# Reordered ACT and DVE work in a self-attention loop, and a reordered first projection, in a fused fp32 Perceiver layer on one core

## The reference

```python
x = x + cross_attention(layernorm(x), ctx)      # 16 heads, 4096 context rows, int8 fake-quant
x = x + self_attention(layernorm(x))            # below
x = x + ffn(layernorm(x))                       # h = silu(gate) * up; out = h @ w_down.T
...
# self-attention: NH, NKV, D = 16, 4, 128; QPG = 4 query heads for each key head
qkv = jnp.einsum('bsh,ph->bsp', x, weight_qkv).reshape(b, s, NKV, GROUP)
scores = jnp.einsum('bsgqd,btgd->bgqst', q, k) * scale
scores = jnp.where(causal, scores, jnp.finfo(scores.dtype).min)
attn = jax.nn.softmax(scores, axis=-1)
out = jnp.einsum('bgqst,btgd->bsgqd', attn, v).reshape(b, s, NH * D)
return jnp.einsum('bse,he->bsh', out, weight_proj)
```

## Time and profile before

| what | value |
|---|---|
| median of 3 runs | 643.45 us (641.19 to 646.16) |
| the profiled execution | 641.48 us |
| its span | 639.7 us (1.78 us lie around it) |
| PE busy | 602.2 us, 94% of the span |
| DVE, ACT, POOL busy | 369.5, 299.4, 228.6 us |
| mean granted TensorE clock | 0.976 of full speed |

### The profile page before, as it was taken

One profiled execution on the slowest core, in us unless ns is written; L12 is line 12 of the kernel. 1 busy time (PEld: TensorE's weight loads), 2 busy tenths in 40 slices (PEclk: granted clock), 3 DMA queues, 4 the chain that ended last, 5 costly groups with the idle time before them and its releaser, 6 DMA issues.

```text
span 639.7 us, 12391 instructions
## 1 busy us (share of the span) xinstructions
PE 602.2 (94%) x4340; PEld 476.6 (75%) x4340; DVE 369.5 (58%) x680; ACT 299.4 (47%) x424; POOL 228.6 (36%) x120
## 2 busy tenths in 40 slices
PE   5999999999999999999999999997697999979998
PEld 3877788888887677777776777764497988769996
DVE  3796621330434778878878777766564334366652
ACT  4435232233231555555555555564247667634441
POOL 2000200000001778888788888870001544400000
PEclk9999999999999999999999999999699899979999
DMA  8664545514529655566555666600130324144510
GB/s 305 228 227 161 173 170 180 191 72 157 203 93 282 165 149 146 147 164 159 153 143 143 158 165 156 156 29 2 26 145 28 132 76 188 67 181 151 196 66 33
DMA packets 29758, 92.17 MB, mean 144 GB/s; under 512 B 5473, under 2 KB 9569, under 8 KB 23009
## 3 DMA queue, kind: packets, MB, share of 16 engines
q1 hardware_dynamic: 28480, 89.67, 45.8%
q10 hardware_dynamic: 1248, 2.10, 0.9%
HBM read 65.02 MB, written 18.35 MB: 130 GB/s over the span
## 4 chain that ended last, share of the span: by engine, by line
PE 87%; DVE 4%; ACT 3%; issue 2%; POOL 1%; DMA 1%; SPq 0%; POOLq 0%; ACTq 0%; DVEq 0%
PE ps L333 17%; PE ps L334 16%; PE ps L335 16%; PE ps L1283 11%; PE ps L1368 9%; PE ps L1380 9%; PE ps L1394 4%; POOL p_sum L574 1%; PE ps L1354 1%; PE ps L1356 1%; DMA f_ring<-stream 1%; PE ps L1549 1%; PE ps L1562 1%; ACT probs L744 1%; PE ps L1265 1%
## 5 line engine op out<-in xcount | busy, mean ns | idle before, releaser
L693 ACT ACTIVATE p_ring<-ps 128x1024 f32<-128x1024 f32 x128 | 125.7, 1022 | 103.1 <-PE ps L1368 76.2
L957 DVE TENSOR_REDUCE m_part<-ps 128x1 f32<-128x512 f32 x240 | 150.5, 684 | 30.7 <-PE ps L1283 27.9
L574 POOL TENSOR_TENSOR p_sum<-p_sum,p_ring 128x1024 f32<-128x1024 f32 x60 | 142.9, 2381 | 9.4 <-ACT p_ring L693 5.3
L1283 PE MATMUL ps<-k_stack,q_max 96*128 96x512 f32 x240 | 87.3, 424 | 1.4 <-issue 0.6
L1368 PE MATMUL ps<-q_stack,k_stack 98*128 98x256 f32 x512 | 81.5, 288 | 0.2 <-ACT p_ring L693 0.2
L1368 PEld LDWEIGHTS ps<-q_stack,k_stack 98*128 98x128 f32 x512 | 75.8, 192 | 7.8 <-ACT p_ring L693 1.2
L1380 PE MATMUL ps<-p_ring,v_head 128*32 128x256 f32 x1024 | 71.6, 383 | 0.1
L333 PE MATMUL ps<-xt_h,h_ring 128*128 128x256 f32 x208 | 60.8, 292 | 2.1 <-DVE xt_l L1071 2.1
L910 DVE SCALAR_TENSOR_TENSOR kl_buf<-ps,biases,kh_buf 128x512 fp32r<-128x512 f32 x32 | 23.9, 749 | 64.0 <-ACT kh_buf L651 63.7
L333 PE MATMUL ps<-h_ring,wkv_h 128*128 128x512 f32 x128 | 52.4, 410 | 8.2 <-DVE l_ring L870 7.2
L334 PE MATMUL ps<-xt_l,h_ring 128*128 128x256 f32 x208 | 60.1, 289 | 0.0
(11 more groups left out here) (186 smaller groups left out, 1032.4 us busy)
## 6 DMA issues: line engine op xcount, KB each, us to landing
f_ring<-stream SPq DMA_DIRECT2D x29, 1024.0 KB, 4.9
k_stack<-kh_scratch SPq DMA_DIRECT2D x60, 256.0 KB, 4.6
kh_scratch<-kh_buf SPq DMA_DIRECT2D x32, 256.0 KB, 5.5
kl_scratch<-kl_buf SPq DMA_DIRECT2D x32, 256.0 KB, 5.8
v_head<-v_all SPq DMA_DIRECT2D x16, 512.0 KB, 3.0
k_stack<-kl_scratch SPq DMA_DIRECT2D x30, 256.0 KB, 4.2
v_all<-stream SPq DMA_DIRECT2D x4, 256.0 KB, 4.6
f_ring<-stream SPq DMA_DIRECT2D x4, 256.0 KB, 5.4
```

The lines of the kernel that those rows point to most:

```text
L574: nc.gpsimd.tensor_tensor(p_sum[:, p, :], p_ring[:, 0, :] if n == 0 else p_sum[:, p, :], p_ring[:, c % 4, :], ALU.add).then_inc(sums_done, 1)
L693: nc.scalar.activation(p_ring[:, c % 4, :], ps[:, 2 * (c % 2):2 * (c % 2) + 2, :].rearrange("p b n -> p (b n)"), ACT.Exp, scale=XSCALE).th ...
L957: nc.vector.reduce_max(m_part[:, j // NT, j % NT:j % NT + 1], maximum_bank(j), AX.X).then_inc(max_read, 1)
L1283: nc.tensor.matmul(maximum_bank(j), q_max[p][0:SPLIT_ROWS, at128(j % NT)], k_stack[p][0:SPLIT_ROWS, j // NT * D:(j // NT + 1) * D], start= ...
```

## The change

There are three edits, and no arithmetic is added or removed.

1. Group 0 only: the high part of the first head's transposed probabilities is put ahead of the first half of the next queries, on ACT and on DVE.
2. Every group but the last: on ACT, `next_query(1)` moves from behind `exponential(3)` to behind `output_high(1)`, so that `normalize(3)`, `transposed_high(2)` and `output_high(1)` come first. In group 0 the second half of the rounding of slot 0 also moves behind `output_high(1)`. On DVE, `next_query(1)` moves behind `invert(3)`, `transposed_low(2)` and `output_low(1)`.
3. PE, the first 12 matmuls after the second and the third layernorm: the passes that read only `xt_h` (eight of them) come first and wait for `xth_ready`; the four that read `xt_l` come last and wait for `xtl_ready`. The sum is taken in another order.

```diff
@@ ACT, group(g)
+                transposed_high(0)
                 if first:
                     next_query(0)
-                transposed_high(0)
                 exponential(2, g)
...
                 if first:
                     half_high(0, 0)
                 exponential(3, g)
+                normalize(3, g)
+                transposed_high(2)
+                output_high(1)
+                if first:
+                    half_high(0, 1)
                 if more:
                     next_query(1)
-                normalize(3, g)
-                if first:
-                    half_high(0, 1)
-                transposed_high(2)
-                output_high(1)
-                if more:
                     half_high(1, 0)
                 else:
                     high(act, FF0, 2, uses(FF0))
@@ DVE, group(g)
+                transposed_low(0)
                 if first:
                     next_query(0)
-                transposed_low(0)
                 maximum(2, g)
...
                 output_low(0)
-                if more:
-                    next_query(1)
                 invert(3, g)
                 transposed_low(2)
                 output_low(1)
                 if more:
+                    next_query(1)
                     maximum(0, g + 1)
@@ PE, project_to_columns(w, u, to, after_norm)
                 for v in range(2):
+                    whole = to[:, v * N:(v + 1) * N]
+                    if after_norm is not None and v == 0:
+                        for kt in range(KT):
+                            if kt % 2 == 0:
+                                pe.wait_ge(xth_ready, 2 * after_norm + kt // 2 + 1)
+                            for part in (h_ring, l_ring):
+                                nc.tensor.matmul(whole, part[w][:, kt, at128(2 * u)], xt_h[:, kt, :],
+                                                 start=kt == 0 and part is h_ring, stop=False)
+                        for kt in range(KT):
+                            if kt % 2 == 0:
+                                pe.wait_ge(xtl_ready, 2 * after_norm + kt // 2 + 1)
+                            nc.tensor.matmul(whole, h_ring[w][:, kt, at128(2 * u)], xt_l[:, kt, :], start=False,
+                                             stop=kt == KT - 1)
+                        continue
                     for kt in range(KT):
-                        if after_norm is not None and v == 0 and kt % 2 == 0:
-                            pe.wait_ge(xtl_ready, 2 * after_norm + kt // 2 + 1)
-                        last = three_pass(to[:, v * N:(v + 1) * N], h_ring[w][:, kt, at128(2 * u + v)],
+                        last = three_pass(whole, h_ring[w][:, kt, at128(2 * u + v)],
```

## The result

The changed kernel ran in 631.83 us (median of 4 runs, 630.79 to 637.08), against 642.91 us for the kernel before (median of 4, 641.19 to 646.16). The ratio is 0.9866, with a 95% interval of 0.9824 to 0.9908. The intervals overlap, so a fair size for the gain is some 7 to 8.6 us, not the 11 us between the first two medians.

A forecast was written before the change was run, and what follows sets the result against it. PE, busy 94% of the span, was taken as the bound, with time won only in its idle or low-clock stretches. Terms 2.8 + 2.2 + 1.1 = 6.1 us against the 643.45 us median gave 637.5 us, range 634.5 to 642.0.

The forecast's parts named there:

- Groups 1 and 2: Fourth head of both groups: the 1.48 us gap goes and values(3) starts 1.41 us earlier, 2.8 us for two groups.
- After the two layernorms: First projections there: PE starts 0.72 us earlier, each gaining 0.36 to 0.72 us, taken as 0.54, together 1.1 us.
- both of my bounds: After both layernorms together: 0.7 us if the clock returns at the same moment, 1.4 us if its return moves along.
- Group 0: Fourth head to first projection: starts 1.63 us earlier, plus 0.56 us from faster matmuls, 2.2 us with the clock up.
- The new start: First projection in group 0: PE starts at about 496.9 us instead of 498.53, a gain of 1.63 us.
- the *new* bound: Group 0's projection meets a new wait for POOL's low part of the weights, whose start moves by only 0.46 us.
- the first rival: Clock still falls in group 0, costing 1.7 to 3.35 us, say 2.5: gain 3.6, time 639.9 us; chance 0.30.
- The head of group 0: Group 0's start: the 0.85 us gap shrinks by some 0.45 us, worth nothing by itself.
- The sum: Whole kernel: 2.8 + 2.2 + 1.1 = 6.1 us with the clock up in group 0; chance 0.48.
- The other rivals: Another wait replaces the removed one, 640.9 us (0.12); gain misses PE's end, 642.3 (0.05); POOL slower, 645.45 (0.05).
- the second rival: values(2) or values(3) gives back half the gap, 640.9 us; sign: 0.5 us wait in groups 1 and 2; chance 0.12.
- 5.3: POOL's subtraction per group: time over 5.3 us is lost in each of three groups, making the kernel slower; chance 0.05.

The follow-up runs named there:

- e2_order: Only the ACT and DVE reordering (edits 1 and 2, edit 3 taken back) against the kernel before: 637.49 us, before 641.07, ratio 0.9938.
- e3_loops: Only edit 2, and only in groups 1 and 2, against the kernel before: 637.39 us, before 641.07, ratio 0.9926.
- l1_fill: Kernel before with 10 unused matmuls of 256 columns in the 1.48 us gap of groups 1 and 2: 640.95 us, before 641.30, ratio 0.9988.
- e1_norm: Only edit 3, PE's pass order after the two layernorms, against the kernel before: 638.01 us, before 641.07, ratio 0.9951.
- g1_pause: Kernel before with 4 unused matmuls of 256 columns in the pause before the first projection after each of both layernorms: 637.39 us, before 641.13, ratio 0.9953.
- g3_keepb: Kernel before with unused matmuls ahead of the cross-attention's output transposes and both layernorms' transposes (12, 12, 10 of 512 columns): 636.99 us, before 641.13, ratio 0.9922.
- g0_fill: Kernel before with 18 unused matmuls of 256 columns in group 0's 2.53 us gap: 640.38 us, before 641.28, ratio 0.9985.
- h2_warm: Changed kernel with unused matmuls in the pauses around both layernorms, ahead of the cross-attention's output transposes and in group 0's three gaps: 628.84 us, ratio 0.9814.
- e4_head: Only edit 1, the exchange at the head of group 0, against the kernel before: 641.90 us, before 641.07, ratio 1.0024.
- h1_warm: Changed kernel with unused matmuls ahead of the cross-attention's output transposes and around both layernorms, group 0 not filled: 629.50 us, ratio 0.9809.

## Why the prediction was wrong, point by point

The step that failed is the pricing of PE's gaps. The terms were sized from where the clock stood in one execution of the kernel before: no fall behind the 1.48 us gaps (2.8 us, too little), a fall behind the 2.53 us gap (2.2 us, too much), and a return behind the layernorms that a pause was taken not to delay (1.1 us, too little). The steps between the engines were right to some tenths of a us.

**Groups 1 and 2: the mechanism held, the term left out the clock.** Every step is in the trace: the copy to `pt_h` waits for PE's transposes, the 1.48 us gap is gone, and the stretch is 2.78 us shorter than in the profile of before, against 2.8. But I took this profile for the usual state of things and wrote that gaps of 0.85 and 1.48 us "brought no fall". In seven profiles with the old order and nothing added in it, this stretch took 41.97, 41.98, 43.27, 43.28, 44.49, 44.83 and 47.65 us, mean 43.9: only two of the seven are free of a fall. With the new order it took 39.13 to 39.19 us in all nine. The profiles put the term at 4.8 us, not 2.8. The times give less, 3.6 to 4.0 us for e2_order and 3.7 to 4.7 for e3_loops, and their intervals hold 4.8. That falls came behind the gap is shown: in five of the seven profiles with it, and in none of ten without it (nine with the new order, and l1_fill). What they cost on average isn't: these seven profiles make it 1.9 us, and l1_fill, which should have won that back, won 0.35 us (at most 2.2). The fault was to set the price of a gap from two copies of it in one execution.

**After the two layernorms: the right step, mis-sized.** I put 0.54 us on each, 0.36 for a return of the clock at the same moment and 0.72 for one that moves with the start. The runs show a return that comes sooner still: 1.8 us less behind the first matmul, on average, than with the pause. Both stretches together took 12.7 to 13.9 us in seven profiles with the pause (mean 13.3) and 9.7 to 11.4 us in four with reordered passes (mean 10.4). By the profiles the term is 2.9 us, not 1.1 (e1_norm: 3.1, between 0.6 and 5.6), and both of my bounds (0.7 and 1.4) lay under it. g1_pause points to the cause: with the pause filled and the work starting no sooner, there is a gain of that size. I had treated the pause as idle time; it was also what kept the clock down. The Trainium skill's rule on transposes ("TensorE: Matmul & The Clock Gate", Part 4) would have given 1.4 us; it pointed the right way and not far enough, and no run here tests it by itself. I also wrote that the clock stays low through the transposes. It fell during them: in the kernel before at 455.4 us, as they began, and at 564.6 us, 1.1 us after they had begun.

**Group 0: the sum looked right and was wrong.** I forecast 2.2 us and the two profiles differ by 1.99. But the old order with the clock up takes 23.98 to 23.99 us (e1_norm, g3_keepb, g0_fill) and the new one 23.70 to 23.72 us (the changed kernel twice, h2_warm). The order is worth 0.3 us, and this stays so with falls counted in: over all profiles in which nothing was added in this group, the means are 25.0 us (seven with the old order) and 24.7 us (six with the new). The new start itself was forecast well: 496.9 us is 19.4 us behind the second `qt_h`, and it came 19.6 us behind it. Wrong was the start that it was set against, 498.53 us, which had a fall in it. I had POOL's chain as the *new* bound and moved it by 0.46 us (it moved by 0.25); it was the bound before as well, hidden in the profile by a slow PE that arrived later than POOL. The rest of the term was the price of the fall, and the fall isn't cured: with the new order and group 0 not filled in, it was there in four of six profiles (25.14 to 25.26 us); with the old one in five of seven. That makes the first rival right in its mechanism: the clock still falls in group 0 in many executions. It costs some 1.5 us there, just under the 1.7 to 3.35 that I gave.

**The head of group 0.** Right: a gap of 0.39 us instead of 0.85, no gain (e4_head).

**The sum.** 2.8 + 2.2 + 1.1 = 6.1 becomes 4.8 + 0.3 + 2.9 = 8.0 us by the profiles, which is between the two comparisons (6.8 us by medians on one chip, 8.6 us by the first ratio); with the smaller size of the first term, 3.7 us, it is 6.9. So two terms were too small and one too large, and the errors don't fully cancel. The rest of the miss is luck: a median of 4 executions with a spread of 6 us fell low. On the second chip the changed kernel's 634.53 us would have been just inside the range. The Trainium skill says that the monitor of activity runs freely and that the number of slow matmuls differs from run to run (the same page, Part 1: What's actually happening). The runs agree: the same kernel took 638.21 to 647.49 us on one chip, and the profiles of kernels with the same code in a stretch differ by where the clock fell. I named this rule for the first rival and didn't apply it to the two terms where it mattered.

**The other rivals.** One wait grew in the gap's place, that at `values(3)`, from 0.11 to 0.49 us, where my steps had 0.07 us more; this is just under the 0.5 us that I had named as the sign of the second rival. It didn't take the gain back, since the transposes ahead of it came 1.6 us sooner instead of 1.48, and `values(3)` 1.37 us instead of 1.41. POOL stayed at 4.6 us and never came near 5.3.

Open: how often the clock falls in each gap (a profile is one execution) and so what the falls in groups 1 and 2 cost on average, where the scatter of some 3 us at one mean clock comes from, and whether the 0.7 us of h2_warm is real.

## What to carry to other kernels

Before a gap of TensorE is priced from one profile, look at the spread of the plain runs together with the mean granted clock of each: here a spread of 9 us came with clocks of 0.965 to 0.979, so the clock fell in some executions and not in others, and a gap is worth its idle time plus its share of these falls. To measure that share, fill the gap with matmuls nobody reads, which moves no true work. And when a stall ends at a slow engine, check whether the wait behind it is set by another chain that the slowness hides; the way to see it is a profile of the same code with the clock up.

## What the runs showed that I had not expected

- A gap of only 1.48 us can bring the clock down: it fell up to 1.8 us behind this gap in at least one of groups 1 and 2 in five of seven profiles. One fall cost 1.3 to 2.9 us (41.97 against 43.27, 43.28 and 44.83), two cost 2.5 and 5.7 us (44.49, 47.65).
- Without that gap the slow tail was missing in e2_order and e3_loops (spreads of 2.2 and 4.3 us over 12 executions; the kernel before, 9.3 us over 35). The changed kernel as a whole still spreads over 6.2 us in 6 executions, so a narrower spread isn't shown for it.
- Added matmuls whose result is unused make the kernel faster: g1_pause by 3.0 us (0.8 to 5.2) with 8 matmuls of 256 columns, and h1_warm by 5.0 us against the changed kernel on the same chip.
